# Starting the first attention group inside the tail of the state-space stage, with its buffers laid out anew

## What is computed

```python
x = _layernorm(x + _L0_attn_ref(x, ...))             # state space
x = _layernorm(x + _L0_xattn_ref(x, ctx, ctx, ...))  # attention over ctx, 16 heads
x = _layernorm(x + _L0_ffn_ref(x, ...))              # 2 of 16 experts
x = _layernorm(x + _L1_attn_ref(x, ...))             # wkv recurrence
x = _layernorm(x + _L1_xattn_ref(ctx, x, ...))
x = _layernorm(x + _L1_ffn_ref(x, ...))              # 6 of 32 experts

# _L0_attn_ref, its end:   return x_ssm * v @ w2_w.T + w2_b
# _L0_xattn_ref, its start:
q = (queries @ Wq.T).reshape(B, S, H, hd)
k = (keys @ Wk.T).reshape(B, S, H, hd)
v = (values @ Wv.T).reshape(B, S, H, hd)
```

## Time and profile before

| | |
|---|---|
| median of 3 runs | 1650.44 us (1649.47 to 1656.49) |
| the profiled execution | 1662.29 us, its span 1660.5 us |
| granted TensorE clock, mean | 0.921 of full speed |
| busy share of the span | PE 84%, PEld 68%, DVE 53%, ACT 36%, POOL 31% |
| HBM traffic | 182.90 MB read, 163.09 MB written, 208 GB/s over the span |

### The profile page before, as it was taken

One profiled execution on the slowest core, in us unless ns is written; L12 is line 12 of the kernel. 1 busy time (PEld: TensorE's weight loads), 2 busy tenths in 40 slices (PEclk: granted clock), 3 DMA queues, 4 the chain that ended last, 5 costly groups with the idle time before them and its releaser, 6 DMA issues. The chain is left out here.

```text
span 1660.5 us, 31310 instructions
## 1 busy us (share of the span) xinstructions
PE 1398.0 (84%) x11403; PEld 1121.0 (68%) x11403; DVE 877.5 (53%) x2509; ACT 590.6 (36%) x1487; POOL 522.5 (31%) x532
## 2 busy tenths in 40 slices
PE   7675888765999999988599997999898747899988
PEld 4463666553999999845378885566566425799986
DVE  6344665545122212148987731357678844566646
ACT  4112333221212221124233222456556411466652
POOL 1001001001111111055444441002445665677664
PEclk9887999876999999999899998999899758999999
DMA  6841977655988887549999991011221598556548
GB/s 162 141 172 52 370 280 306 265 214 206 366 328 321 327 336 278 190 140 267 261 265 256 256 210 66 13 39 64 78 84 59 209 343 274 177 179 179 177 146 331
DMA packets 163888, 348.12 MB, mean 210 GB/s; under 512 B 12704, under 2 KB 122928, under 8 KB 158224
## 3 DMA queue, kind: packets, MB, share of 16 engines
q1 hardware_dynamic: 139904, 285.73, 54.2%
q0 software_dynamic: 15888, 43.52, 7.3%
q10 hardware_dynamic: 7936, 16.78, 3.2%
HBM read 182.90 MB, written 163.09 MB: 208 GB/s over the span
## 5 line engine op out<-in xcount | busy, mean ns | idle before, releaser
L155 PE MATMUL bank<-arena 128*128 128x128 f32 (+9 forms) x11403 | 1398.0, 324 | 255.3 <-DVE arena L155 107.6
L155 PEld LDWEIGHTS bank<-arena 128*128 128x128 f32 (+5 forms) x11403 | 1121.0, 174 | 531.9 <-issue 221.7
L155 ACT ACTIVATE arena<-bank 128x512 f32<-128x512 f32 (+3 forms) x636 | 270.8, 461 | 623.7 <-PE bank L155 603.7
L155 POOL TENSOR_TENSOR arena<-arena 128x512 f32<-128x512 f32 (+5 forms) x188 | 185.4, 986 | 666.0 <-DVE arena L155 450.8
L155 ACT ACTIVATE arena<-bank,arena 128x256 f32<-128x256 f32 (+3 forms) x494 | 206.3, 456 | 178.9 <-PE bank L155 142.2
L155 DVE TENSOR_SCALAR arena<-bank,arena 128x128 f32<-128x128 f32 (+1 forms) x212 | 69.8, 384 | 275.7 <-PE bank L155 267.0
L155 ACT ACTIVATE arena<-arena 128x256 f32<-128x256 f32 (+7 forms) x225 | 118.0, 580 | 262.3 <-DVE arena L155 228.9
L155 POOL DMA_INDIRECT ys<-arena x146 | 150.6, 1032 | 88.5 <-ACT arena L155 71.9
L155 DVE TENSOR_TENSOR arena<-bank,arena 128x128 f32<-128x128 f32 (+5 forms) x331 | 124.0, 388 | 101.0 <-PE bank L155 76.5
L155 DVE COPY arena<-bank 128x256 f32<-128x256 f32 (+2 forms) x136 | 76.5, 579 | 140.5 <-PE bank L155 140.5
L155 DVE TENSOR_TENSOR arena<-arena 128x512 f32<-128x512 f32 (+17 forms) x306 | 111.0, 385 | 19.1 <-POOL arena L155 10.4
(11 more groups left out here) (22 smaller groups left out, 149.9 us busy)
## 6 DMA issues: line engine op xcount, KB each, us to landing
arena<-in_bank SPq DMA_DIRECT2D x41, 2052.0 KB, 10.6
xs<-arena SPq DMA_DIRECT2D x32, 2193.0 KB, 28.5
xsa<-arena SPq DMA_DIRECT2D x16, 2193.0 KB, 9.3
arena<-xs SPq DMA_DIRECT2D x114, 129.0 KB, 2.2
arena<-in_bank SPq DMA_DIRECT2D x8, 1536.0 KB, 21.6
arena<-ys SPq DMA_DIRECT2D x16, 768.0 KB, 8.7
arena<-kd SPq DMA_DIRECT2D x16, 512.0 KB, 10.2
kvd<-arena ACTq DMA_DIRECT2D x16, 512.0 KB, 7.8
```

The costliest lines, as they stand in the source:

```text
L155: ins = fn(*a, **kw)
```

## The change

The barrier behind `phase_b` is taken out. Instead the state of T, V, A and G after `state_space` is noted as `calm`; S, V, A and G wait for it, and the two context loads and `h_sel` are issued right behind. `pipeline` gets a fifth item, `part(first, 6)`, which lets the first six steps of `pre_c(0)` be recorded in rounds 4 to 9, interleaved with the last steps of `phase_b`. Then POOL, in place of DVE, clears `none`, one `Vb` tile and the `mq` tiles; `h_tail` waits for `none`; the barrier stands here; POOL clears the other `Vb` tile; and the last two steps of `pre_c(0)` run.

The layout of the attention buffers is split in four ranges. What group 0 needs before the new barrier (`ctxb`, `cT`, the first `kT`, and the first `qm`) lies over the Toeplitz half of `P`, `tmpA`, `K`, `xcT` or the conv and Toeplitz buffers, all done at `calm`. What lies over `W0`, the `z` half of `P`, `vT` and `ssm`, which `phase_b` still reads (`oT`, `mT`, `rc`, some `pe`, the second `qm`, `Vb` and `kT`, `cnb`), is used behind the new barrier. The sizes and numbers of all buffers stay.

```diff
-        pipeline([phase_b(g) for g in range(4)])
-        barrier()
+        calm = [(e.sem, e.n) for e in (T, V, A, G)]
...
-        top[0], limit[0] = marks[1], 50912
+        top[0], limit[0] = marks[1], marks[0] + 2048
+        oT = Slots([alloc(1024) for _ in range(2)])
...
+        top[0], limit[0] = marks[0] + 2048, marks[0] + 8752
         none = alloc(1462)
-        V(v.memset, none, 0.0, free=True)
+        ctxb = Slots([alloc(1024) for _ in range(2)])
+        cT = Slots([alloc(1024) for _ in range(2)])
+        kT = [alloc(1024)]
+        top[0], limit[0] = marks[0] + 8752, marks[0] + 16944
+        qm, Vb = [alloc(2048)], [alloc(2048)]
...
+        top[0], limit[0] = marks[0] + 16944, 50912
+        qm = Slots([alloc(2048), *qm])
+        Vb = Slots([alloc(2048), *Vb])
...
-        h_tail = S.dma(s.dma_start, ys0[...], view(none, ...), Lane(sem()), w=[(V.sem, V.n)])
...
-        for i in range(2):
-            vb, _ = Vb.get()
-            h = V(v.memset, vb, 0.0, free=True)
-            Vb.put(vb, h)
-        for i in range(3):
-            b, _ = mq.get()
-            h = V(v.memset, b, 0.0, free=True)
-            mq.put(b, h)
...
+        def part(steps, n):
+            for _ in range(n):
+                next(steps)
+                yield
+
+        for e in (S, V, A, G):
+            e.wait(*calm)
         for g in range(2):
             load_c(g)
-        for _ in pre_c(0):
+        h_sel = S.dma(s.dma_start, sel, ins["sel"], Lane(sem()))
+        first = pre_c(0)
+        pipeline([phase_b(g) for g in range(4)] + [part(first, 6)])
+        h_none = G(p.memset, none, 0.0, free=True)
+        h_tail = S.dma(s.dma_start, ys0[...], view(none, ...), Lane(sem()), w=[h_none])
+        for ring in (Vb, mq):
+            for i in range(1 if ring is Vb else 3):
+                b, _ = ring.get()
+                h = G(p.memset, b, 0.0, free=True)
+                ring.put(b, h)
+        barrier()
+        b, _ = Vb.get()
+        Vb.put(b, G(p.memset, b, 0.0, free=True))
+        for _ in first:
             pass
```

More of the change, by code:

```diff
@@ L560, in build @@
         h_xd = []
-        top[0], limit[0] = marks[1], 50912
-        none = alloc(1462)
-        V(v.memset, none, 0.0, free=True)
+        top[0], limit[0] = marks[1], marks[0] + 2048
+        oT = Slots([alloc(1024) for _ in range(2)])
+        mT = Slots([alloc(128) for _ in range(2)])
+        rc = Slots([alloc(256) for _ in range(2)])
+        pe = [alloc(512)]
+        top[0], limit[0] = marks[0] + 2048, marks[0] + 8752
+        none = alloc(1462)
+        ctxb = Slots([alloc(1024) for _ in range(2)])
[3 more added lines that the diff above has]
+        qm, Vb = [alloc(2048)], [alloc(2048)]
+        kT = Slots([*kT, alloc(1024)])
+        cnb = Slots([alloc(1024)])
+        pe += [alloc(512) for _ in range(4)]
+        top[0], limit[0] = marks[0] + 16944, 50912
+        qm = Slots([alloc(2048), *qm])
+        Vb = Slots([alloc(2048), *Vb])
+        pe = Slots(pe + [alloc(512) for _ in range(3)])
+        mq = Slots([alloc(128) for _ in range(3)])
+        sel = alloc(576)
         xs1 = nc.dram_tensor("xs1", [(32 * 17 + 1) * 128, ROWX], F32, kind="Internal").ap()
@@ L568, in build @@
         ys0 = nc.dram_tensor("ys0", [NT0 * 128, 256], F32, kind="Internal").ap()
-        h_tail = S.dma(s.dma_start, ys0[LIKELY0 * 128:, :].rearrange("(p k) f -> p (k f)", p=128), view(none, 0, [[0, NT0 - LIKELY0], [1, 256]]), Lane(sem()), w=[(V.sem, V.n)])
         fl = [Lane(sem()) for _ in range(3)]
@@ L579, in fill_zeros @@
                 h_fill.append(S.dma(s.dma_start, to, view(src, 0, [[0, k], [1, width]]), fl[len(h_fill) % 3], w=[w]))
[L581 to L592, removed]
         cnd = nc.dram_tensor("cnd", [2048, 256], F32, kind="Internal").ap()
@@ L595, in build @@
         h_cn = []
-        sel = alloc(576)
-        h_sel = S.dma(s.dma_start, sel, ins["sel"], Lane(sem()))
         clane = [Lane(sem()) for _ in range(2)]
-        for i in range(2):
-            vb, _ = Vb.get()
-            h = V(v.memset, vb, 0.0, free=True)
-            Vb.put(vb, h)
-        for i in range(3):
-            b, _ = mq.get()
-            h = V(v.memset, b, 0.0, free=True)
-            mq.put(b, h)
         def softmax_block(bk, h, nh, nk, m, mo):
@@ L856, in nothing @@
             yield
+        def part(steps, n):
[4 more added lines that the diff above has]
+            e.wait(*calm)
         for g in range(2):
             load_c(g)
-        for _ in pre_c(0):
+        h_sel = S.dma(s.dma_start, sel, ins["sel"], Lane(sem()))
+        first = pre_c(0)
+        pipeline([phase_b(g) for g in range(4)] + [part(first, 6)])
+        h_none = G(p.memset, none, 0.0, free=True)
+        h_tail = S.dma(s.dma_start, ys0[LIKELY0 * 128:, :].rearrange("(p k) f -> p (k f)", p=128), view(none, 0, [[0, NT0 - LIKELY0], [1, 256]]), Lane(sem()), w=[h_none])
+        for ring in (Vb, mq):
[7 more added lines that the diff above has]
+        for _ in first:
             pass
```

## The result

Over 20 runs of each, the changed kernel takes 1642.46 us (1634.52 to 1653.74) and the kernel before 1654.39 (1645.5 to 1661.55). The ratio is 0.9934 with a 95% interval of 0.9913 to 0.9955: faster by 10.9 us, with 7.4 to 14.4 as bounds. The forecast was a gain of 15.9 us and a time of 1634.5 us, in a range from 1629.5 to 1642.0.

A forecast was written before the change was run, and what follows sets the result against it. A chain of waits bounds 120 to 160 us. Waits of 6.7 + 7.0 and 3.2 + 0.9 + 0.9 of half clock go, 1.8 of pause and 0.9 of barrier return: 15.9 off 1650.44 gives 1634.5 us, range 1629.5 to 1642.

The forecast's parts named there:

- PE's wait for the normalisation: End of `phase_b`: PE's wait for group 3's normalisation, 6.71 us, would be removed.
- its wait for the context: Ahead of the context transposes: PE's wait for the context DMA, 6.98 us, would be removed.
- the pause in their place: Ahead of the first q: PE would wait 2.6 us for DVE's context copies, queued behind group 3's statistics.
- POOL's memsets: Ahead of the new barrier on POOL: 3.7 us, ending near 139.5, 3.8 us ahead of the barrier.
- the power behind the bias addition: On POOL: group 3's power, behind group 0's bias addition, would end at 135.65 instead of 135.0, hidden under q.
- ACT's normalisation: Beside the first q: group 3's normalisation, 2.08 us, stays hidden; ACT's last q copy ends near 142.1, DVE's at 143.3.
- `calm` on POOL: In `phase_b`: the first two `hb` additions, held back to near 108, end at 110.4 and 112.9, the first with 1.7 us of cover.
- step 3 of the sum: Behind the new pause: q, k, q, k at 1.72 us each, ending at 142.5.
- rival A: The clock falls in the pause ahead of q: gain 12.7 us, time 1637.7; chance 0.25.
- B: At the new barrier: POOL is last because its memsets are slower; gain 14.6 us, time 1635.8; chance 0.03.
- C: Before the context transposes: the context is late after all, 1642 us or more; chance 0.09 with D's milder half.
- D: Attention loop pays back 9 us (1643.5; 0.09 with C) or 24 us (1658.5; 0.03), at most 1.5 us an iteration.

The follow-up runs named there:

- e4: The changed kernel with 20 unused transposes on PE between the context transposes and the first q; ratio to the kernel before 0.9881.
- e2: The changed kernel, unedited, run again; ratio to the kernel before 0.9921.
- e5: The changed kernel with the first group's preparation begun one round sooner, in the round of group 3's first step; ratio to the kernel before 0.9909.
- e6: The changed kernel with 20 small matmuls ahead of PE's first work; ratio to the kernel before 0.984.
- e12: The changed kernel with 20 small matmuls ahead of PE's first work, a second time on another chip; ratio to the kernel before 0.986.
- e1: The kernel before, unedited, run again; ratio to the kernel before 1.0013.
- e10: The changed kernel, unedited, a fourth time, on the last chip; 1697.24 us, ratio to the kernel before 0.9905.
- e11: The changed kernel with the first group's preparation begun one round sooner, a second time; ratio to the kernel before 0.9896.
- e7: The kernel before with 20 small matmuls ahead of PE's first work; ratio to the unedited kernel before 0.9921.

## Why the prediction was partly right

**Right: the waits and nearly all terms.** PE's wait for the normalisation and its wait for the context are gone; the pause in their place was forecast at 2.6 us and is 2.94; POOL's memsets, the power behind the bias addition, ACT's normalisation and SP's queue stayed hidden, ACT with 1.15 us ahead of DVE's last copy (1.2), POOL with 6.35 ahead of the barrier (3.8); the barrier cost 0.8 us (0.9). With the clock held up (e4) the sum is met to 0.1 us: 15.8 against 15.9. `calm` on POOL stayed hidden too: in e2 the two additions that it holds back run from 108.12 to 112.98 (forecast: 108 to 112.9), and `phase_b` takes 22.20 us as before.

**Wrong: step 3 of the sum, "q, k, q, k at 1.72 each".** The sum kept the clock at full behind the new pause, 6.9 us for the four projections. They took 8.80 in all four profiles of the changed kernel, because the clock fell just after q had begun; e4 and e5, with pauses of 0.80 and 1.15 us, have 7.10 and 7.11. This possibility stood beside the sum as rival A, with too small a weight and too high a price. The fall of the clock in the pause had a chance of 0.25, against a row that showed a fall without any longer pause. It came in all four profiles, and in e6 and e12. It also cost 1.65 us, not 3.2: I took the price from the kernel before, where PE worked at half clock from the start of q at 149.28 to about 155.3, while here it did so from about 135.8 to 139.2 (both by the mean clocks of the stretches of 2 us). The likeliest case should have been 14.2 us. The sentence drawn from the Trainium skill ("TensorE: Matmul & The Clock Gate", section "Part 1: The HAM clock gate"), that the judged stretch is not aligned with the kernel, was taken to mean that the fall would come and go between runs. The traces agree that the moment of the fall moves (about 1.2 us after the start of q in the first profile, 0.5 in e2, by the mean clocks of 0.95 and 0.56 in their stretches of 2 us), and that its cost can move with it (1.36 us in e12, where it came 0.6 us ahead of q). A fall that comes and goes between runs of one program was seen, but at the first `w2` matmuls and not in this pause.

**Wrong: the base, and with it the range.** The absolute forecast stood on a median of three runs, 1650.44; over 20 runs the same kernel has 1654.39. Of the 8.0 us by which the forecast missed, 4.0 are that, and 1.65 are the clock. Had either of the two been right, the time would have lain inside the range. What is left, 2.4 us, is less than the half-width of the measurement, 0.0021 of 1654, or 3.5 us, so it needs no cause; the clock in `phase_b`, which the sum left as it was, is one that would give as much. Had the range allowed for a base that three runs fix no better than to their own spread of 7 us, it would have held the time.

**Not so: B, C and D.** POOL idles 6.35 us ahead of the barrier (B), no PE wait names the context (C), and the loop is as long as before (D, three profiles more). The price in D was also misread: the step of 11.43 us ran at a mean granted clock of 1.00, and what made it longer is in the main a stop of PE at issue, 1.11 us up to 305.60, which every kernel without added matmuls has at this place.

**Not seen at all:** that executions of one and the same program differ by some 15 us in head and tail. Of the 6.6 us between the heads of the kernel before and e1, 4.9 are PE's stops at issue (10.6 and 5.7 us in all); the 7.0 us of the tail were not taken apart. I had taken the difference between the profiled execution and the median, 11.85 us, as nothing to do with the stretch, which was right, but did not ask where it sat.

## What to carry to other kernels

When a stage boundary is a barrier with idle engines around it, write down which chain ends last on each side, put the next stage's loads ahead of the barrier, and weave its first steps into the last rounds; here that gave 14 us of 1654 in the trace, a little over half by the load and the rest by the overlap. Then look at the pause that remains on TensorE: one of 2.94 us let the clock fall every time, those of 0.80 and 1.15 us in the same place did not, and another order of the same steps can be what removes it. Elsewhere pauses of 0.7 to 1.1 us, a few in a row, saw it fall in some executions and not in others (the `w2` matmuls of e10 and e2). Judge such a change by the distance between two marks in the trace, which repeated to 0.01 us in four profiles of the changed kernel and to 0.07 in two of the kernel before, look at what lies just outside the marks as well, and leave the whole time to many runs.

## What the runs showed of the hardware

PE stops at fixed counts of its instruction stream, with no wait that the profile shows: 0.5 to 1.7 us in the attention loop, while the zero fills keep the DMA share of most of these steps near 1.0, and up to 5.8 us in the state-space stage (e11). 20 matmuls of 32x32 at the start of the program move these stops, and moved the time by 13.4 us in the kernel before (ratio 0.9921) and by 9 to 11 us in the changed one, more than most edits of the work itself.

The traces show what ends these stops. The page of the changed kernel lists a DMA queue of kind instruction (packets, MB, share):

```profile
q8 instruction: 94, 1.54, 0.4%
```

Each packet of it is 16 KB, and the trace has the time of each. In the changed kernel one runs from 326.22 to 327.10, and PE is back from its stop at 328.46; in e12 one runs from 157.33 to 158.21, and PE is back at 159.78. In all 14 profiles, up to the end of the loop, PE has 79 idle times of 0.45 us or more that are put down to issue, other than the pause ahead of q and one of 3.57 us in the sixth iteration, which stays in its place in every kernel. All 79 end 1.2 to 1.6 us after such a packet has landed, and none of the others does. So PE waits there for its next instructions. Why the packet comes too late at these places and in time at others is not shown. That other DMA traffic holds it back is an inference; a kernel with the fills taken away would test it and was not run.

In e6, e7 and e12 the 20 also put PE to work sooner after the start, but up to 60 us into the span e10 and e12 stand within a microsecond of each other, so the head is not shortened there.
